# Four transformer layers on one core: opening as one block by quarters, loads issued ahead, output by quarters, the last layer's norm inside its block

## What is computed

```python
def _layernorm(x, axis=-1, eps=1e-05):
    m = jnp.mean(x, axis=axis, keepdims=True)
    v = jnp.var(x, axis=axis, keepdims=True)
    return (x - m) / jnp.sqrt(v + eps)
...
    x = L0_attn_x
    xn = _layernorm(x, axis=-1)
    x = x + _L0_attn_ref(xn, ...) + _L0_ffn_ref(xn, ...)
    xn = _layernorm(x, axis=-1)
    x = x + _L1_attn_ref(xn, ...) + _L1_ffn_ref(xn, ...)
    xn = _layernorm(x, axis=-1)
    x = x + _L2_attn_ref(xn, ...) + _L2_ffn_ref(xn, ...)
    xn = _layernorm(x, axis=-1)
    x = x + _L3_attn_ref(xn, ...) + _L3_ffn_ref(xn, ...)
    return x
```

```python
        def fp4_quant_dequant(x):
            xb = x.reshape(shape[:-1] + (shape[-1] // BLOCK, BLOCK))
            scale = jnp.max(jnp.abs(xb), axis=-1, keepdims=True) / 6.0
            scale = jnp.maximum(scale, jnp.float32(1e-12))
            xn = xb / scale
            idx = jnp.searchsorted(_MID, jnp.abs(xn))
            q = _GRID[idx] * jnp.sign(xn) * scale
            return q.reshape(shape)
        gate = fp4_linear(x, w_gate)
        y = fp4_linear(x, w_up)
        h = jax.nn.silu(gate) * y
        return fp4_linear(h, w_down)
```

## Time and profile before

| | us |
|---|---|
| median of 3 runs | 1824.28 |
| lowest and highest run | 1817.33, 1830.55 |
| the profiled execution, its own time | 1828.21 |
| its span in the profile | 1826.5 |
| PE, DVE, ACT, POOL busy | 1686.7, 1314.1, 1240.6, 107.7 |

### The profile page before, as it was taken

How to read it: one execution, slowest core, us unless ns; L and a number is a source line. 1 busy time by engine, 2 the same in 40 slices (tenths; PEclk the granted TensorE clock), 3 DMA queues, 4 the chain that set the end, 5 groups by cost and what they waited for, 6 DMA issues and landing times. The chain is left out here.

```text
span 1826.5 us, 19512 instructions
## 1 busy us (share of the span) xinstructions
PE 1686.7 (92%) x6936; PEld 695.3 (38%) x6944; DVE 1314.1 (72%) x1815; ACT 1240.6 (68%) x1607; POOL 107.7 (6%) x151
## 2 busy tenths in 40 slices
PE   5699999999999999997999799997898999897998
PEld 2133333333333333332444366553233333333665
DVE  4677777777777777761433238865999999995997
ACT  2488888888888888885434376344886757762663
POOL 1000111111100111021000100000000000000000
PEclk7799999999999999999899889998999999998999
DMA  3400101010000100001331121120444534441000
GB/s 117 122 6 13 24 13 24 12 24 12 18 18 7 30 1 12 7 1 47 61 69 58 34 60 48 40 41 14 141 153 155 167 133 165 146 156 35 1 1 24
DMA packets 52026, 100.79 MB, mean 55 GB/s; under 512 B 8151, under 2 KB 21558, under 8 KB 51780
## 3 DMA queue, kind: packets, MB, share of 16 engines
q1 hardware_dynamic: 51930, 99.54, 18.7%
HBM read 91.55 MB, written 7.87 MB: 54 GB/s over the span
## 5 line engine op out<-in xcount | busy, mean ns | idle before, releaser
L785 DVE TENSOR_REDUCE best<-quad 128x2 f32<-128x1024 f32 x256 | 309.7, 1221 | 130.4 <-PE quad L575 128.0
L699 ACT ACTIVATE weights<-quad 128x1024 f32<-128x1024 f32 x256 | 255.4, 1027 | 28.9 <-PE quad L600 28.5
L108 PE MATMUL quad<-xn,l_w1s 128*128 128x512 f32 x288 | 150.4, 630 | 11.5 <-DMA l_w2s<-in_F_w 7.1
L2545 ACT ACTIVATE l_hid<-quad,l_w1s 128x512 f32<-128x512 f32 x112 | 74.9, 686 | 98.9 <-PE quad L108 98.2
L617 PE MATMUL quad<-weights,values 128*32 128x512 f32 x1024 | 136.4, 605 | 0.4 <-ACT weights L699 0.4
L2407 PE MATMUL quad<-l_st,ident 128*128 128x512 f32 x256 | 119.4, 594 | 5.8 <-DVE l_st L2611 5.8
L108 PE MATMUL quad<-q,wf 128*128 128x512 f32 x256 | 121.5, 607 | 0.7 <-DVE mk L756 0.3
L2453 PE MATMUL quad<-l_hid,l_w2s 128*128 128x512 f32 x224 | 109.0, 621 | 14.0 <-DVE l_hid L2642 14.0
L108 PE MATMUL quad<-hid,wf 128*128 128x512 f32 x256 | 116.6, 599 | 0.0
L643 ACT ACTIVATE hid<-quad,col 128x512 f32<-128x512 f32 x128 | 84.7, 686 | 21.7 <-PE quad L108 21.5
L108 PE MATMUL quad<-sq_all,mean_w 128*128 128x512 f32 x176 | 95.8, 642 | 1.8 <-ACT sq_all L1334 0.9
(11 more groups left out here) (384 smaller groups left out, 3025.2 us busy)
## 6 DMA issues: line engine op xcount, KB each, us to landing
l_bs<-xd_dram SPq DMA_DIRECT2D x32, 512.0 KB, 5.1
l_c_rows<-xd_dram SPq DMA_DIRECT2D x32, 512.0 KB, 4.9
l_cs<-comb SPq DMA_DIRECT2D x28, 512.0 KB, 4.8
end_cs<-comb SPq DMA_DIRECT2D x32, 256.0 KB, 3.9
l_cs<-comb SPq DMA_DIRECT2D x32, 256.0 KB, 3.4
wf<-in_L_f SPq DMA_DIRECT2D x16, 256.0 KB, 2.7
l_w1s<-in_F_w SPq DMA_DIRECT2D x28, 129.0 KB, 2.1
l_w2s<-in_F_w SPq DMA_DIRECT2D x28, 128.0 KB, 2.2
```

What stands on the lines that cost most here:

```text
L108: last = nc.tensor.matmul(out[:, c:c + BANK], lhsT, rhs[:, c:c + BANK], start=(n == 0), stop=(n == len(pairs) - 1))
L699: nc.scalar.activation(weights[p % BUFS][:, slot, :, :].rearrange("p a t -> p (a t)"), doubles.of("weigh", m, i), ACT.Exp, scale=scale).th ...
L785: nc.vector.tensor_reduce(heads[:, :, slot, qt, c], doubles.of("search", m, i).rearrange("p (a t) -> p a t", a=2), AX.X, ALU.max).then_inc ...
L2545: nc.scalar.activation(hid[j % HIDS][:, f, :], ring.of("hidden", j, f), ACT.Gelu, bias=w1s[p][:, F + f:F + f + 1]).then_inc(hidden_read, 1)
```

## The change

**Opening.** `start` and `attention_inputs` become one block, `inputs`. All weights that it and the eight blocks' first step need are issued right behind the four loads of `x`. Queries and keys are made by quarters, as soon as a quarter is normalised. ACT now makes the first bf16 part straight from PSUM and the second from the remainder; DVE makes the remainder in one instruction (L967 in the new file) and the third part (L973). The parts of half 1 lie in `qs1`, `ks1`, `qs2` and `ks2`, the buffers of sets 1 and 2; SP stores them in the next block, behind the loads of set 0, and loads sets 1 and 2 behind that.

**Loads ahead.** The weights for layer 1's projections are issued in `layer_0_end`, those of layer 2's in the norm block before it, and all of layer 3's at the end of layer 2's SP list. Layer 1's router weights become the first load of its block.

**Layer 3.** Its norm moves from a block of its own into `layer_3_branches` as generators (`centres`, `variances`, `squares`, `inverse_roots`, `normalise`), beside the rounding of the gate and up weights. The output goes out by quarters from layer 3's SP list; `finish` is gone.

**Tables.** The numbers of layers 1 and 3 (`PLAN_HALF`, `PLAN_TILE`, `PLAN_EXPERT`, `PLAN_CAUSAL`, `PLAN_PIECE`, `PLAN_FP4`, and the new `PLAN_LAST_NORM`) are replaced, so the order inside these two layers is another. Those of layers 0 and 2 are kept.

```diff
-def attention_inputs(core, w_qk, w_v, cols, v_bias, q_dram, k_dram, values, later, w_out, out_dram, out_w):
...
+def inputs(core, x_in, loads, weights, stacks, full, values, later, w_out, out_dram, out_w):
...
+        @block.sync
+        def _(sp):
+            for c in range(QUARTERS):
+                sp.dma_start(quarter(core.x, c), quarter(x_in, c)).then_inc(x_landed[c], 16)
+            loads(sp)
...
+            for p, done in enumerate((first_done, second_done, third_done)):
+                for i in range(2):
+                    sp.wait_ge(done, 2 + i + 1)
+                    stacks.store(sp, 0, i, p)
+            sp.wait_ge(stacks.stored[0], stacks.all_stored)
...
+            centre(0)
+            centre(1)
+            norm.variance(pe, 0)
+            centre(2)
+            norm.variance(pe, 1)
+            centre(3)
+            norm.variance(pe, 2)
+            queries_and_keys(0)
+            norm.variance(pe, 3)
+            queries_and_keys(1)
+            queries_and_keys(2)
+            pe.wait_ge(weights.v_landed, 32)
+            attention_values(0)
+            queries_and_keys(3)
+            attention_values(1)
...
+            norm.scale(dve, 0)
+            norm.scale(dve, 1)
+            norm.scale(dve, 2)
+            rest(0)
+            norm.scale(dve, 3)
+            rest(1)
+            third(0)
+            rest(2)
+            third(1)
+            rest(3)
+            third(2)
+            attention_values(0)
+            third(3)
+            attention_values(1)
...
-                sp.dma_start(wa[:, :], w_att[0]).then_inc(att_landed, 16)
-                sp.dma_start(col[:, :, :], cols).then_inc(cols_landed, 16)
                 load_set(0)
                 sp.dma_start(wf1[:, :], w_f1[0]).then_inc(f1_landed, 16)
                 sp.dma_start(wf2[:, :, :], w_f2[0]).then_inc(f2_landed, 16)
                 sp.wait_ge(ones_set, 1)
-                for i in range(BUFS):
-                    for par in range(2):
-                        row = 64 * par + ROWS
-                        sp.dma_start(ks[i][row:row + 1, :, :], ones[:, :]).then_inc(ones_landed, 16)
-                load_set(1)
-                load_set(2)
+                load_ones(0)
+                for p in range(3):
+                    for i in range(2):
+                        stacks.store(sp, 1, i, p)
+                sp.wait_ge(stacks.stored[1], stacks.all_stored)
+                for n in range(1, BUFS):
+                    load_ones(n)
+                    load_set(n)
...
-                sp.dma_start(wt[:, :], a["A1_tok"]).then_inc(landed, 16)
-                sp.dma_start(wq[:, :], a["A1_qk"]).then_inc(landed, 16)
+                routing.load(sp)
                 sp.dma_start(wo[:, :], a["A1_wo"]).then_inc(wo_landed, 16)
...
-    "xT": ((-140.280,), (-2.996,)),
-    "q": ((-246.066,), (-93.228,)),
+    "xT": ((-786.213,), (-596.869,)),
+    "q": ((-763.892,), (-569.285,)),
...
+                for r in range(QUARTERS):
+                    sp.wait_ge(net_joined, r + 1)
+                    sp.dma_start(quarter(out, r), quarter(core.x, r)).then_inc(stored, 16)
+                sp.wait_ge(stored, 16 * QUARTERS)
...
+                def normalise():
+                    for c in range(QUARTERS):
+                        yield norm_at("scaled", c)
+                        dve.wait_ge(rstd, c + 1)
+                        nc.vector.tensor_tensor(quarter(core.xn, c), ring.of("norm", c, 0)[:, 0:BANK], quarter(core.sq_all, c), ALU.mult).then_inc(normalised, 1)
```

More of the change, by code:

```diff
@@ L218, in vector, with residual_norm @@
     def vector(self, dve):
         for c in range(QUARTERS):
-            dve.wait_ge(self.rstd, c + 1)
-            self.nc.vector.tensor_tensor(quarter(self.core.xn, c), self.banks[c][0], quarter(self.core.sq_all, c), ALU.mult).then_inc(self.scaled, 1)
-def start(core, x_in):
+            self.scale(dve, c)
+def residual_norm(core, name, ahead):
     nc = core.nc
-    x_landed, built = [core.sem(f"x_landed{c}") for c in range(QUARTERS)], core.sem("constants_built")
-    norm = QuarterNorm(core, "start_norm")
+    norm = QuarterNorm(core, name)
@@ new lines, with __init__, store @@
+class Stacks:
+    def __init__(self, core, q_dram, k_dram, qs, ks, first):
+        self.drams, self.orders = (q_dram, k_dram), (Q_PARTS, K_PARTS)
+        self.part = [first, [[stack[1][:, 0, :], stack[1][:, 1, :], stack[2][:, 0, :]] for stack in (qs, ks)]]
+        self.stored = [core.sem(f"stacked{h}") for h in BOTH]
+        self.all_stored = 2 * TERMS * 16
+    def store(self, sp, h, i, p):
+        rows = self.drams[i][h].rearrange("g j (t d) x -> t (g j) d x", d=HD)
+        for t in range(TERMS):
+            if self.orders[i][t] == p:
+                sp.dma_start(rows[t], self.part[h][i][p]).then_inc(self.stored[h], 16)
@@ L1226, in _ @@
                 sp.dma_start(col2[:, :], a["F0_ln2"]).then_inc(cols_landed, 16)
+                ahead.load(sp)
                 def combine_rows():
@@ L2201, with layer_2_branches @@
 }
-def layer_2_branches(core, a, scratch):
+def layer_2_branches(core, a, scratch, ahead, last):
     nc = core.nc
@@ L2351, in _ @@
                          expert_weights(), combine_rows())
+                last.load(sp)
             @block.gpsimd
@@ L2996, in _, with logs, squares, inverse_roots @@
                 table = [None]
+                def logs():
+                    if table[0] != LN_EXP:
+                        nc.scalar.preload_act_table_set(LN_EXP)
+                    table[0] = LN_EXP
+                def squares():
+                    for c in range(QUARTERS):
+                        yield norm_at("square", c)
+                        act.wait_ge(centred, c + 1)
+                        nc.scalar.activation(quarter(core.sq_all, c), ring.of("norm", c, 0)[:, 0:BANK], ACT.Square).then_inc(squared, 1)
+                def inverse_roots():
+                    for c in range(QUARTERS):
+                        yield norm_at("root", c)
+                        logs()
+                        act.wait_ge(var_ready, c + 1)
+                        nc.scalar.activation(quarter(core.sq_all, c), ring.of("norm", c, 0)[:, BANK:2 * BANK], ACT.Ln, bias=core.eps[1e-5][:, :]).then_inc(log_done, 1)
+                        act.wait_ge(log_done, c + 1)
+                        nc.scalar.activation(quarter(core.sq_all, c), quarter(core.sq_all, c), ACT.Exp, scale=-0.5).then_inc(rstd, 1)
                 def queries_or_keys(h, name, ready, to, read):
@@ new lines, in layer_0, with loads @@
+            qs, ks = ([sb(f"{n}{i}", [P, 2, T], BF16) for i in range(BUFS)] for n in ("qs", "ks"))
+            with ExitStack() as first:
+                weights = InputWeights(core, first)
+                full = [[core.sb(f"full{c}{i}", [P, QUARTER], F32, first) for i in range(2)] for c in range(QUARTERS)]
+                parts = [[core.sb(f"part{i}{p}", [P, T], BF16, first)[:, :] for p in range(3)] for i in range(2)]
+                stacks = Stacks(core, q_dram, k_dram, qs, ks, parts)
+                def loads(sp):
+                    weights.load(sp, a)
+                    sp.dma_start(wa[:, :], a["L0_att"][0]).then_inc(att_landed, 16)
+                    sp.dma_start(col[:, :, :], a["L0_cols"]).then_inc(cols_landed, 16)
+                inputs(core, a["x"], loads, weights, stacks, full, values, later, w_out, a["F0_out"], out_w)
```

658 lines of the change are left out of this document (351 added, 307 removed).

## The result

The changed kernel takes 1763.64 us (median of 4 runs, 1762.13 to 1769.45) against 1824.78 before (the median of 4 runs as well, one more than stands on record above): ratio 0.9673, 95% interval 0.9632 to 0.9715. Later, on another chip, the same two kernels gave 1768.31 and 1825.18, 57 us, ratio 0.9697 (0.9672 to 0.9722).

The account below looks back on a forecast made before the run. PE, 92% busy, was read as busiest, with gains sought in waits at stage borders: 25.8 + 3.2 + 2.9 + 12 + 0.9 + 1.8 = 46.6 us off 1824.28 gave 1777.7, rounded to 1778; range 1767 to 1792.

Parts of the forecast that it names:

- Layer 1: Layer 1: PE starts 3.2 us earlier with router weights loaded first; the new order counts 0.
- the 2.1 us of layer 2: Layer 2's first ten matmuls: 2.1 us more if PE stays at 2.4 GHz; not counted in the sum.
- Opening: Kernel start to the eight blocks' first matmul: PE starts at 31.0 instead of 56.79, 25.8 us gained, bounds 22 to 27.
- the stores are hidden by about 1 us: Opening: DVE sets the block's end, at 30.6, and the last store lands by 29.5.
- Layer 2: Layer 2's start: weights loaded in the norm's block remove PE's 2.7 us wait; 2.9 us gained with DVE's.
- Layer 3 and the end: Layer 3: loads ahead and norm beside rounding gain 12 us (8 to 15.5); one quarter of final matmuls left gains 0.9.
- The output: Kernel end: four quarter DMAs instead of one shorten the tail from 5.4 to 4.0 us or less; 1.8 us gained.
- The estimate beside it: Output by the skill page: a quarter lands in 2.6 us, the whole in 4.4, making the term 2.3 us.
- More than the borders: Whole kernel: layer 2's clock 2.1, DVE's 14.8 in layer 3, layer 1's order 3; 54.5 us gained, 1770, chance 0.12.
- PE keeps layer 3 and the new orders cost: Layers 1 and 3: layer 3 gives only 8, layer 1's order loses 3; 39.6 us gained, 1785, chance 0.14.
- slower: Layer 1: the new order leaves tile chains bare, costing about 5 us a tile, 80 in all; 1858, chance 0.02.
- The stores still bound the opening: Opening: late parts make stores end the block at 37.4, 6.8 us later; 1785, chance 0.08.

Follow-up runs that it names:

- run 3: The kernel before with only layer 1's new order tables put in: 1816.37 us, ratio 0.9949.
- run 9: The kernel before, unedited, profiled a second time: 1823.01 us.
- Run 7: The changed kernel with half 1's twelve stores back in the opening's block, behind half 0's: 1774.31 us, ratio 0.9751.
- Run 5: The changed kernel with layer 3's old tables and the last norm ahead of everything, loads still ahead: 1766.56 us, ratio 0.9699.
- run 12: The changed kernel with layer 1's router weights loaded a block earlier and two pairs of projections ahead of the router's matmuls: 1761.79 us, ratio 0.9660.
- run 4: The kernel before with 16 added 128x512 matmuls among layer 1's two groups of 32 small ones: 1835.33 us, ratio 1.0054.

## Why the prediction was wrong

**Layer 1 is the step that failed.** I wrote that "the row shows 5 us of PE idle in 156, so at most 5 to win, and I allow 4 to lose. I take 0." Two things were wrong in it. The row begins at 1060 us; the layer's first 38 us were not looked at, and a window over them in the profile before has 7 us of idle time more (5.0 of it the wait for the router's weights) and a clock of 0.77:

```profile
1022.54:1060.00 37.46, 30.33 (x96) 18.40 (x96) 9.94 (x25) 18.36 (x18) 4.92 (x31) 0.77 0.26 61
```

And its clock column, 0.95, was read past: PE busy for 151 us at 0.95 holds some 8 us that a steady clock gives back, so idle time was no bound on the gain. The layer gave 15.6 us in the profiles against 3.2. The loads' 3.2 came out exactly. The order's idle time gave 4.3 more (tables alone: 6 to 13 us in the medians of run 3, clock included), and the rest, 8.1, was clock: some 1.8 with the earlier start and some 6.9 in the fall behind the first small group, both estimates by the table above, 0.6 over in sum. Of the 8.1, 5.4 us is only the difference between two executions of the kernel before (run 9): against that profile the layer's gain is 10.0 to 10.3 us. So the step that failed is the term of layer 1, sized at 3.2 us with nothing for the order and nothing for the clock; it measured 10 to 15.6, and a good part of the span between the two is luck of the execution.

**The clock as a term.** I let it count in layer 3 only and kept the 2.1 us of layer 2 out. PE's busy time fell by 21.3 us over the whole kernel. The 30 timings of the kernel before beside these experiments run from 1817.1 us at a mean clock of 0.969 to 1832.7 at 0.957, with a correlation of -0.94: most of its scatter goes with the clock. A sum made against one profile carries that scatter: the profile of before was 3.4 us above its median and that of after was the fastest of its four, so the profiles differ by 66.1 us where the medians differ by 61.1 and, on another chip, by 56.9.

**Opening.** Forecast start 31.0, measured 29.44 (28.99 to 30.21 in nine profiles with this opening), so 27.4 us against 25.8, just over my upper bound of 27. DVE was done at 28.30, 1.3 us before what I had called the earliest (29.6); 0.6 of that is the third scale, which starts at 14.02 in place of 14.66. The last store was issued at 25.22, as forecast (25.4), and "the stores are hidden by about 1 us" was wrong only because DVE was early: they set the block's end by 0.8 us. Run 7 prices the twelve moved stores at 10 us. What was moved behind cost nothing, as forecast: the loads of set 2 are issued by 51.3 us, and layer 0's branches and end are no longer than before.

**Layer 2.** The start gave 2.7 us as forecast (2.75 us from the block's start to its first matmul before, 0.05 now). The clock did not stay up there in this execution: the ten matmuls took 7.48 us, at a clock of 0.61, where they had taken 6.51 at 0.73. The stage gained 4.0. PE's busy time in it fell by 1.8, but this is DVE's stage, and where the 1.3 us above the start's come from was not traced.

**Layer 3 and the end.** 15.4 us against 12.9, within the bounds (8 and 15.5, and 0.9 for the last quarter). Run 5 splits them into 10.7 and 4.7. Of the 15.4, 5.2 are PE's busy time, where I had counted 2.3 of clock. What the norm's products among the comparisons and the table load cost was not told apart. The output gave 1.7 against 1.8. The estimate beside it, by the Trainium skill, page "DMA: Bandwidth & Descriptors", section "Anatomy of one DMA", uses a fit that the section gives for DMAs issued by gpsimd, and these are SP's; the measured landings, 2.4 and 3.9 us, are 0.2 and 0.5 below it.

**The rivals.** "More than the borders" (1770, 0.12) came nearest, but not part by part: layer 3 gave nearly DVE's lead and the order more than its 3 us, while the clock at layer 2 did not stay up, and layer 1's clock was in none of its parts. "PE keeps layer 3 and the new orders cost" fell with layer 3's 15.4 us and run 3, "slower" with run 3. "The stores still bound the opening" was right that they end last, by 0.8 us and not by 6.8. The range failed because its lower end held that rival's 3 us for the order and nothing for the clock of layer 1.

## What to carry to other kernels

Read a PE-bound stage by three numbers, not one: idle time, busy time and granted clock, over the whole stage, its first microseconds included; busy x (1 - clock) is an estimate of the time that a change can give back or take without touching any instruction (in layer 1 it is 16 us before and 8 after, and the busy time fell by 8.1). When a profile is the base of a sum, take a second one of the same kernel, or the timings' own clocks, to see which stage's busy time repeats. Behind a border at which the clock has fallen, try the wide matmuls first and the small ones behind them: in run 12 that raised the clock of the first 20 us to 0.91, though its gain in the whole is not clear of the scatter.

## What the hardware showed that I had not expected

- At layer 1's start 32 router matmuls of 8 columns took 6.96 us at the granted 1.2 GHz, and did not bring the clock back; behind eight wide rows they took 3.63 us at 2.4 GHz (run 12).
- The clock falls while PE is busy without a gap (10.00 of 10.00 us at 0.83 in run 9), behind groups of 32 matmuls of 4 columns: behind the second group in all thirteen profiles without added matmuls, behind the first in some. With a wide matmul behind every second small one it stayed at 1.00 (run 4, one profile).
- How far it falls differs between executions: the same layer 1 code had PE busy for 195.2 to 203.6 us. The Trainium skill, page "TensorE: Matmul & The Clock Gate", section "What's actually happening", says that the number of matmuls at the lower clock at a kernel's start varies between runs of one kernel; here the traces show such a difference in the middle of a kernel, by up to 8 us in a layer.
- Twelve stores more in front of a border cost 10.2 us, more than twelve issues at 0.65 us (7.8): the first three of them took 2.73 us to issue and all twelve 9.3, and this execution's first twelve ended 0.8 us later as well.
